# Window attention: the projection as five split float32r products instead of two float32 ones

## The reference, cut to what matters

```python
h = _layernorm(xw, ln1_g, ln1_b)                  # xw: (windows, 64, 192)
qkv = (h @ qkv_w).reshape(-1, N, 3, nh, hd)
q, k, v = (qkv[:, :, 0], qkv[:, :, 1], qkv[:, :, 2])
attn = jax.nn.softmax(jnp.einsum('bnhd,bmhd->bhnm', q, k) * scale, axis=-1)
o = jnp.einsum('bhnm,bmhd->bnhd', attn, v).reshape(-1, N, C)
a = o @ proj_w + proj_b + xw                      # the projection
```

## Time and profile before

| | us |
|---|---|
| median of three runs | 3452.77 (3448.55 to 3457.2) |
| the profiled execution | 3452.14 |
| its span, first to last instruction | 3450.4 |
| mean granted TensorE clock | 0.982 |
| PE busy over the span | 3299.2 (96%) |
| PEld | 3199.6 (93%) |
| DVE | 2625.2 (76%) |
| ACT | 2016.5 (58%) |
| POOL | 1149.2 (33%) |

### The profile page before, as it was taken

The page is one execution under the profiler, slowest core; times in us unless marked ns, Lnnn a source line. Parts: engine busy times, 40 slices in busy tenths (PEclk is TensorE's granted clock), DMA queues, the critical chain, the costliest instruction groups (busy, mean ns, idle before and its releaser), DMA issues. The chain is left out here.

```text
span 3450.4 us, 86941 instructions
## 1 busy us (share of the span) xinstructions
PE 3299.2 (96%) x31288; PEld 3199.6 (93%) x31288; DVE 2625.2 (76%) x6465; ACT 2016.5 (58%) x5410; POOL 1149.2 (33%) x2151
## 2 busy tenths in 40 slices
PE   7999999999799999999978869999999899999999
PEld 6999998899799999999978869989999899989999
DVE  6777777777467676767679989979999788875554
ACT  5777777777344444444436656668999655532222
POOL 4333333333244444444323300014444356630000
PEclk9999999999899999999989989999999999999999
DMA  2677888711012111212178866645555788877775
GB/s 67 183 237 237 259 283 271 254 56 46 22 50 55 48 53 48 56 44 56 48 201 258 265 186 186 199 130 161 169 166 165 211 235 234 236 223 231 226 223 175
DMA packets 473215, 556.40 MB, mean 161 GB/s; under 512 B 78805, under 2 KB 332122, under 8 KB 472794
## 3 DMA queue, kind: packets, MB, share of 16 engines
q1 hardware_dynamic: 447450, 531.57, 51.7%
q10 hardware_dynamic: 25344, 19.27, 1.7%
HBM read 405.31 MB, written 258.67 MB: 192 GB/s over the span
## 5 line engine op out<-in xcount | busy, mean ns | idle before, releaser
L1468 PE MATMUL PS<-dw_grid,dw_mats 128*128 128x196 f32 (+1 forms) x3840 | 627.3, 327 | 34.2 <-DVE dw_mats L1400 34.2
L1468 PEld LDWEIGHTS PS<-dw_grid,dw_mats 128*128 128x128 f32 x3840 | 626.5, 192 | 34.6 <-issue 34.6
L1283 PE MATMUL PS<-mlp_w,mlp_hid 128*128 128x192 f32 x2352 | 414.4, 326 | 0.5 <-ACT mlp_hid L820 0.5
L1396 DVE COPY dw_grid<-X 32x392 f32<-32x392 f32 (+1 forms) x480 | 290.0, 604 | 163.8 <-PE PS L1468 149.6
L1283 PEld LDWEIGHTS PS<-mlp_w,mlp_hid 128*128 128x128 f32 x2352 | 378.6, 190 | 0.8 <-ACT mlp_hid L820 0.8
L1823 PE MATMUL PS<-grn_gain,down_hi 128*128 128x384 f32 x1176 | 353.2, 362 | 10.3 <-POOL X_low L1776 10.3
L820 ACT ACTIVATE mlp_hid<-PS,mlp_b 128x256 f32<-128x256 f32 x588 | 247.5, 472 | 112.1 <-PE PS L811 112.1
L546 ACT ACTIVATE att_vbd<-PS,att_rs 64x96 f32<-64x96 f32 x784 | 264.7, 338 | 12.7 <-DVE att_rows L476 5.4
L1776 POOL TENSOR_TENSOR X_low<-X,down_hi 128x128 fp32r<-128x128 f32 x196 | 208.9, 1066 | 152.5 <-ACT down_hi L1786 152.5
L1134 POOL COPY X<-mlp_x 128x192 f32<-128x192 f32 x196 | 114.7, 585 | 432.5 <-DVE mlp_x L1210 432.0
L1435 ACT ACTIVATE dw_res<-PS,dw_brow 128x196 f32<-128x196 f32 x192 | 81.8, 426 | 298.2 <-PE PS L1468 298.2
(11 more groups left out here) (254 smaller groups left out, 9805.2 us busy)
## 6 DMA issues: line engine op xcount, KB each, us to landing
scratch_hid<-hid_hid SPq DMA_DIRECT2D x196, 320.0 KB, 3.4
down_hid<-scratch_hid SPq DMA_DIRECT2D x196, 320.0 KB, 3.6
scratch_wide<-scratch_taps SPq DMA_DIRECT2D x64, 960.0 KB, 6.1
dw_raw<-scratch_wide SPq DMA_DIRECT2D x96, 640.0 KB, 4.3
scratch_wide<-scratch_taps SPq DMA_DIRECT2D x64, 768.0 KB, 5.5
dw_raw<-scratch_wide SPq DMA_DIRECT2D x96, 512.0 KB, 3.6
scratch_u<-mlp_u SPq DMA_DIRECT2D x56, 378.0 KB, 3.0
att_x<-in_x SPq DMA_DIRECT2D x196, 96.0 KB, 2.3
```

The costliest lines, as they stand in the source:

```text
L1283: last = nc.tensor.matmul(psD[i], hid[:, p.buf(2), m, i * 128:(i + 1) * 128], w2[:, m, :], start=(m == 0), stop=(m == MC - 1))
L1396: last = nc.vector.tensor_copy(dst, src)
L1468: last = nc.tensor.matmul(dst[:, :, ys, :], m, src, start=(i == 0), stop=(i == len(steps) - 1))
```

## The change

The projection is computed from rounded parts. `oh` is `ot` rounded to float32r, `ol` is the rest, and the weights are split in the same way (`wpa` for channels 0 to 127, `wpb` for the other 64). Channels 128 to 191 stand twice in the transposed tile, in partitions 0 to 63 and again in 64 to 127: GpSimd copies these 64 columns of `o` beside themselves (`twice`) so that one product with `wpb` gives high x high and high x low at once. The fifth product has the low part of these channels in partitions 0 to 63, and two rows of ones (64 and 96) against two rows of `wpr`, the bias and its rest. The rounding and splitting is GpSimd's (`halves`). `ot`, `oh` and `ol` have one buffer each, and `xt` has two instead of three. GpSimd now works in every step. The weights' split is made by VectorE in a new function `projection()` at the end of its step 4, and not before the loop. The raw weights and bias are loaded with five DMAs instead of two.

```diff
-    XR, TR = 12, 3
+    XR, TR = 12, 2
...
-    o = s.sb("o", [128, 2, C])
-    ot = s.sb("ot", [128, 2, KC, 128])
+    o = s.sb("o", [128, 2, 256])
+    ot = s.sb("ot", [128, 256])
+    oh = s.sb("oh", [128, 256], F32R)
+    ol = s.sb("ol", [128, 256], F32R)
...
-            sp.dma_start(wp[0:CH, :, :], a["L0_conv_proj_w"].rearrange("(k p) n -> p k n", k=KC)).then_inc(wloaded, 16)
-            sp.dma_start(pbrow[96:97, :], a["L0_conv_proj_b"].partition_broadcast(1)).then_inc(wloaded, 16)
+            for at_, rows_, k in ((slice(0, 128), slice(0, 128), 0), (slice(0, 64), slice(128, C), 1), (slice(64, 128), slice(128, C), 1)):
+                sp.dma_start(wp[at_, k, :], a["L0_conv_proj_w"][rows_, :]).then_inc(wloaded, 16)
+            for r in (64, 96):
+                sp.dma_start(pbrow[r:r + 1, :], a["L0_conv_proj_b"].partition_broadcast(1)).then_inc(wloaded, 16)
...
+            def halves(b):
+                pool.wait_ge(q["ot_ready"], b.n + 1)
+                if b.reached(1):
+                    pool.wait_ge(q["proj"], b.n)
+                else:
+                    pool.wait_ge(q["ones"], 2)
+                nc.gpsimd.tensor_copy(oh[:, :], ot[:, :]).then_inc(q["o_high"], 1)
+                pool.wait_ge(q["o_high"], b.n + 1)
+                nc.gpsimd.tensor_tensor(ol[:, 0:128], ot[:, 0:128], as_f32(oh[:, 0:128]), ALU.subtract).then_inc(q["o_low"], 1)
+                pool.wait_ge(q["o_low"], b.n + 1)
+                nc.gpsimd.tensor_tensor(ol[0:64, 128:256], ot[0:64, 128:256], as_f32(oh[0:64, 128:256]), ALU.subtract).then_inc(q["o_split"], 1)
+                pool.wait_ge(q["o_split"], b.n + 1)
+
+            def twice(b):
+                pool.wait_ge(q["o_ready"], b.n + 1)
+                nc.gpsimd.tensor_copy(o[:, b.buf(2), C:256], o[:, b.buf(2), 128:C]).then_inc(q["o_twice"], 1)
...
+            def body(t):
+                b = t.back(AHEAD + 4)
+                if b.inside(NB):
+                    halves(b)
+                b = t.back(AHEAD + 3)
+                if b.inside(NB):
+                    twice(b)
+                if t.inside(NB) and t.j % 2 == 0:
+                    columns(t.pair())
+                if t.inside(NB) and t.j % 2 == 1:
+                    spread(t)
+            unrolled(NB, LAG, body)
...
-                dve.wait_ge(q["pbias"], 1)
-                nc.vector.tensor_tensor(wp[96:97, 0, :], psPB, pbrow[96:97, :], ALU.add).then_inc(q["weights"], 1)
-                dve.wait_ge(q["weights"], 1)
                 dve.wait_ge(q["split"], 2)
+
+            def projection():
+                for i, r in enumerate((64, 96)):
+                    dve.wait_ge(q["pbias"], 1)
+                    nc.vector.tensor_tensor(pbrow[r:r + 1, :], psPB[i], pbrow[r:r + 1, :], ALU.add).then_inc(q["pb"], 1)
+                nc.vector.tensor_copy(wpa[0][:, :], wp[:, 0, :]).then_inc(q["pw"], 1)
...
+                if t.n == 4:
+                    projection()
...
-                    if b.reached(2):
-                        act.wait_ge(q["proj"], b.n - 1)
-                    nc.scalar.activation(ot[0:CH, b.buf(2), :, :], psOT.rearrange("p (k n) -> p k n", k=KC), ACT.Identity).then_inc(q["ot_ready"], 1)
+                    if b.reached(1):
+                        act.wait_ge(q["o_split"], b.n)
+                    nc.scalar.activation(ot[:, :], psOT, ACT.Identity).then_inc(q["ot_ready"], 1)
...
-                    pe.wait_ge(q["o_ready"], b.n + 1)
+                    pe.wait_ge(q["o_twice"], b.n + 1)
...
-                    for k in range(KC):
-                        last = nc.tensor.transpose(psOT[:, k * 128:(k + 1) * 128], o[:, b.buf(2), k * CH:(k + 1) * CH], ident[:, :])
-                    last.then_inc(q["ot"], 1)
+                    nc.tensor.transpose(psOT[:, 0:128], o[:, b.buf(2), 0:128], ident[:, :])
+                    nc.tensor.transpose(psOT[:, 128:256], o[:, b.buf(2), 128:256], ident[:, :]).then_inc(q["ot"], 1)
...
-                    pe.wait_ge(q["ot_ready"], b.n + 1)
+                    pe.wait_ge(q["o_split"], b.n + 1)
...
-                    nc.tensor.matmul(psPJ, ot[0:CH + 1, b.buf(2), 0, :], wp[0:CH + 1, 0, :], start=True, stop=False)
-                    nc.tensor.matmul(psPJ, ot[0:CH, b.buf(2), 1, :], wp[0:CH, 1, :], start=False, stop=True).then_inc(q["proj"], 1)
+                    else:
+                        pe.wait_ge(q["weights"], 5)
+                    terms = ((oh[:, 0:128], wpa[0][:, :]), (oh[:, 0:128], wpa[1][:, :]), (ol[:, 0:128], wpa[0][:, :]), (oh[:, 128:256], wpb[:, :]),
+                             (ol[0:97, 128:256], wpr[0:97, :]))
+                    for j, (h, w) in enumerate(terms):
+                        last = nc.tensor.matmul(psPJ, h, w, start=(j == 0), stop=(j == 4))
+                    last.then_inc(q["proj"], 1)
```

More of the change, by code:

```diff
@@ L296, in attention @@
     wb = s.parts("wb", [128, W])
-    wp = s.sb("wp", [128, KC, C])
+    wpa = s.parts("wpa", [128, C])
+    wpb = s.sb("wpb", [128, C], F32R)
+    wpr = s.sb("wpr", [128, C], F32R)
     gb = s.sb("gb", [128, 2, 2])
     qkbias = s.sb("qkbias", [128, QK])
-    vbias = s.sb("vbias", [CH, KC])
+    vbias = s.sb("vbias", [128, KC])
     ident = s.sb("ident", [128, 128])
@@ L335, in attention @@
     psMean = [PS[:, i, 0:HALF] for i in range(2)]
-    psVB = PS[0:CH, 7, 0:KC]
-    psPB = PS[96:97, 4, 0:C]
+    psVB = PS[:, 7, 0:KC]
+    psPB = [PS[r:r + 1, 4, 0:C] for r in (64, 96)]
     wloaded, ready, loaded, tloaded = s.sem("wloaded"), s.sem("ready"), s.sems("loaded", 4), s.sems("tloaded", TR)
@@ L341, in attention @@
              "stats", "aggr", "var_ok", "rstd", "h_high", "h_low", "h_ready", "half_a", "half_b", "a_kept", "b_kept", "v_ready",
-             "turned", "qk_ready", "scores", "max", "shifted", "probs", "pt", "pt_ready", "pv", "recip", "o_ready", "ot", "ot_ready",
+             "turned", "qk_ready", "scores", "max", "shifted", "probs", "pt", "pt_ready", "pv", "recip", "o_ready", "ot", "ot_ready", "o_high", "o_low", "o_split", "o_twice", "pb", "pb_high", "pw", "ones",
              "proj", "resid")
     q = {x: s.sem(x) for x in names}
-    LOADS = 3 + 6 + 1 + 1
+    LOADS = 3 + 6 + 3 + 2
     READY = 6 + 4 * 2
@@ L394, in _ @@
             pool.wait_ge(ready, 4)
-            nc.gpsimd.memset(ot[96:97, :, 0, :], 1.0).then_inc(ready, 1)
+            nc.gpsimd.memset(zeros, 0.0).then_inc(ready, 1)
             pool.wait_ge(ready, 5)
@@ L401, in _, with columns @@
             pool.wait_ge(ready, 6)
-            def body(t):
-                if t.j % 2 == 0 or not t.inside(NB):
-                    return
-                u = t.pair()
+            def halves(b):
[13 more added lines that the diff above has]
+                nc.gpsimd.tensor_copy(o[:, b.buf(2), C:256], o[:, b.buf(2), 128:C]).then_inc(q["o_twice"], 1)
+            def columns(u):
                 if u.n == 3:
@@ L420, in body, with spread @@
                 pool.wait_ge(q["h_ready"], u.n + 1)
+            def spread(t):
+                u = t.pair()
                 both = slice(t.buf(4) - 1, t.buf(4) + 1)
@@ L564, in _ @@
             pe.wait_ge(q["wide"], 1)
-            for k in range(KC):
-                m = slice(QK + k * CH, QK + k * CH + CH)
-                nc.tensor.matmul(psVB[:, k:k + 1], raw[:, 0, m], gb[:, 1, 0:1], start=True, stop=False)
-                nc.tensor.matmul(psVB[:, k:k + 1], raw[0:64, 1, m], gb[0:64, 1, 1:2], start=False, stop=True)
+            for k, n in ((0, 128), (1, 64)):
+                m = slice(QK + k * 128, QK + k * 128 + n)
+                nc.tensor.matmul(psVB[0:n, k:k + 1], raw[:, 0, m], gb[:, 1, 0:1], start=True, stop=False)
+                nc.tensor.matmul(psVB[0:n, k:k + 1], raw[0:64, 1, m], gb[0:64, 1, 1:2], start=False, stop=True)
             for out, m in ((psA, slice(0, HALF)), (psB[:, 0:QK - HALF], slice(HALF, QK))):
@@ L578, in _ @@
             last.then_inc(q["mean"], 1)
-            pe.wait_ge(q["bias_kept"], 1)
-            for k in range(KC):
-                last = nc.tensor.matmul(psPB, vbias[:, k:k + 1], wp[0:CH, k, :], start=(k == 0), stop=(k == KC - 1))
+            pe.wait_ge(q["bias_kept"], 2)
+            for out in psPB:
+                nc.tensor.matmul(out, vbias[:, 0:1], wp[:, 0, :], start=True, stop=False)
+                last = nc.tensor.matmul(out, vbias[0:64, 1:2], wp[0:64, 1, :], start=False, stop=True)
             last.then_inc(q["pbias"], 1)
             pe.wait_ge(q["centred"], 4)
-            pe.wait_ge(q["weights"], 2)
+            pe.wait_ge(q["weights"], 1)
             pe.wait_ge(q["split"], 2)
```

26 lines of the change are left out of this document (21 added, 5 removed).

## The result

| | before | after |
|---|---|---|
| median, us (6 runs each, one chip) | 3454.29 (3447.49 to 3458.18) | 3471.17 (3465.59 to 3476.54) |
| ratio | | 1.0052, 95% interval 1.0037 to 1.0068 |
| span of the profiled execution | 3450.4 | 3467.9 |

A forecast was written before the change was run, and what follows sets the result against it. The prediction took TensorE to bound attention. From the profiled 3452.1 us it took 22.6 for shorter steps and added 9.8 paid once, giving 3439.3, so a median of 3440, range 3420 to 3455.

The forecast's parts named there:

- the paragraph on SP: SP's DMA queue: `xt` loads issued about 4.7 us later, still over 12 us before use; nothing booked.
- the paragraph on GpSimd: GpSimd in attention: load 3.4 of 4.14 us per block, TensorE's copy 1.3 us to spare; nothing booked.
- The products: TensorE's projection: five float32r products at 0.112 us shorten each step by 0.12 us, 22.6 us over 188 steps.
- Rival A: TensorE's projection: stationary operand loads hide, five products cost 0.09 us each; 3423 us, chance 0.18.
- Rival C: GpSimd bounds every step, its two subtractions slowed by contention to 1.10 us each; 3592 us, chance 0.07.
- What is paid once: Set-up and pipeline filling: 1.1 set-up, 3.0 `projection()`, 4.2 GpSimd insertions, 1.5 clock; 9.8 us in all.
- The set-up: Before the loop: three more DMA issues delay the start, less L455 leaving its end; cost 1.1 us.
- the two insertions on GpSimd: GpSimd's steps 6 and 10: clearing of tables costs about 2.4 us, preparation about 1.8, together 4.2.
- the clock: TensorE's start: three new stalls, each with one chance in three of about 1.7 us at lower clock; 1.5 booked.
- Rival B: Gain spent: products at 0.116 us each, start costs 12 to 15 us through lower clock; 3450 to 3453, chance 0.17.

The follow-up runs named there:

- e2: The changed kernel with each expansion issued right behind the load of `x`, ahead of the `xt` loads: 3444.0 us, ratio 0.9976 to before.
- e16: e4 with the load of a pair's `xt` moved a step later on SP: 3428.1 us, ratio 0.992 to before.
- e17: The changed kernel with only the load of `xt` moved a step later on SP: 3452.43 us, ratio 1.0002 to before.
- e3: The changed kernel with table clearing, table preparation and most of the weights' split moved to earlier places: 3464.92 us, ratio 1.0034 to before.
- e5: The kernel before with both expansions of a pair of steps issued back to back in the odd step: 3467.66 us, ratio 1.0033.
- e15: e12 with the changed kernel's GpSimd work added on a tile of its own, for which nobody waits: 3485.05 us, ratio 1.0086 to before.
- e12: The kernel before with e2's order on SP and two `xt` buffers instead of three: 3446.3 us, ratio 0.9977.
- e7: The changed kernel with all 128 expansions issued after the loop of attention: 3746.57 us, ratio 1.0841 to before; only attention is compared.
- e13: e4 with a sixth product in the projection: 3452.8 us, ratio 0.9997 to before.
- e4: The changed kernel with the edits of e2 and e3 together: 3437.42 us, ratio 0.9954 to before.

## Why the prediction was wrong

**The step that failed** is the paragraph on SP, "Nothing is booked". It looked at what the delayed load of `xt` and the loads of `x` are needed for, and both were in time indeed. It did not list the expansions among what is queued behind the new wait, nor ask what their bunching would disturb. Nor did the paragraph on GpSimd follow its new place of the rounding, 6.5 us after the step's start, into SP's wait. What the runs showed in its place: the excess rose from 11.7 to 40.8, 29 us of a miss of 31; the start has 1.0 more (below), and the steps 0.8. Changes to SP's order and waits show the cause: e2, e16 and e17 on the changed kernel (-27, and -43 with e3's edit, and -19), e5 and e15 on the kernel before (+14, and +39 over e12, of which 6 are a stop at 128 us), and e7, in which the changed kernel does not stop from 135 us on until its expansions start, at 827. That a late piece of the program is the link between the two is read from the DMA records beside each stop; no run changed it by itself.

**The products** came out as forecast: 0.116 us a step against 0.12, with 0.11 a product. The parts of the sum were less exact than the sum: the group starts 0.13 us behind the first transpose (0.22 was booked), its first distance is 0.17 and not 0.11, and from the last product to L695 pass 0.21 (0.18). TensorE: Matmul & The Clock Gate, a page of the Trainium skill, gives about P/1.2 ns for a load of P columns (section LDWEIGHTS), an estimate of 107 ns here; by that the loads set the pace, and the 108 to 113 ns agree, while the 82.5 ns, which the page gives for a product alone (section Back-to-back issue gap), do not appear. Rival A is out.

**GpSimd** was right in its sizes, 0.455 and 0.449 against 0.46, and in that TensorE never waits for it in a full step. Rival C is out. Its busy time in the 200 us is 137.3; 140 was forecast.

**What is paid once** was forecast at 9.8. TensorE's step 14 starts at 68.79 us before and at 81.66 after; with the six short steps until then the changed kernel has paid 13.6. But the kernel before pays in its steps 14 to 16 for VectorE's tables and for the low clock of the earlier trace rows. By step 17 (86.82 and 96.56), nine short steps included, 10.8 are left, 1.0 over the forecast, and e3, which starts step 17 at 85.99, takes 10.6 of them back. The set-up cost 0.9 (1.1). Behind `projection()` TensorE waited 3.66 (3.0), and behind the two insertions on GpSimd 2.17 and 1.54, together 3.7 (4.2):

```profile
39.55 1.12 PE L719 MATMUL PS<-att_ident,att_rows 128*128 128x128 f32 x4 [3.66 <-DVE att_rows L531]
```

```profile
53.32 0.33 PE L671 MATMUL PS<-att_ident,att_o 128*128 128x128 f32 x1 [2.17 <-POOL att_o L426]
...
73.14 0.33 PE L671 MATMUL PS<-att_ident,att_o 128*128 128x128 f32 x1 [1.54 <-POOL att_o L426]
```

The rest is 5.3 us at step 14 and 2.5 at step 17, against 1.5 booked for the clock; no run separates what the clock has in it. Each of the three stalls came with a stretch at the lower level, where one chance in three had been booked (windows as in the earlier trace rows; before, only the third place had one):

```profile
38.00:42.00 4.00, 2.45 (x11) 2.45 (x12) 3.15 (x9) 2.39 (x6) 0.94 (x2) 0.50 0.14 42
42.00:46.00 4.00, 4.00 (x66) 3.60 (x64) 2.39 (x7) 2.33 (x7) 0.44 (x4) 0.70 0.09 24
54.00:57.00 3.00, 3.00 (x58) 2.69 (x58) 2.19 (x6) 1.66 (x6) 2.41 (x7) 0.61 0.30 80
...
75.00:78.00 3.00, 3.00 (x33) 2.93 (x15) 2.65 (x7) 1.78 (x4) 2.70 (x7) 0.52 0.15 38
```

**Rival B** (the gain is spent) came nearest, but stopped 18 us short of the result and had the start as its reason and not SP. A slower kernel had 0.10 of the chances, for other reasons. With both mended, e16 against e12, two buffers of `xt` and no gap under 3.2 us in both, the change is worth 18 of the 22 us that the products were to bring: step 195 starts at 833.79 against 852.79.

**Open** is why the same number of close pairs costs more in one kernel than in another: 63 cost before 27 us, 41 cost after 41, 48 cost e15 36. In the latter two an `xt` load and an `x` load leave in the same burst. Nor do the records show what delays a piece of code, only that it comes late. That the short step or denser code (D) counts as well where the expansions are crowded is suggested by e13 and not shown. The four kernels with no gap under 3.2 us have 4.5 to 5.5 us, whatever their code, step or buffers, which leaves D little room where SP is even.

## What to carry to other kernels

When a change delays an engine, follow every semaphore of that engine into the DMA queue, and list all that is queued behind the wait, above all large background transfers that nobody seems to wait for. Put a load that waits for late work behind the transfers that need no wait, and a step later, so that the queue is paced by one wait a step; either alone left 17 to 19 us of excess here (e2, e4, e17), both together 5.5 (e16). Where TensorE stops at "issue" in a run of products without semaphores, look for its cause among the DMAs: here it was the program itself arriving late.

## What was not expected of the hardware

This long unrolled program is fetched while it runs, TensorE's in 257 pieces of 16 KB before and 259 after, and large data transfers issued close together hold it up. The average DMA share told nothing: from 400 to 600 us e16 moves more than after, 294 GB/s against 269 (0.90 against 0.81), and does not stall. Trainium Architecture — The Big Picture, a page of the Trainium skill (section The software stack), tells of instruction streams brought to the engines at load; here they come during the run, one piece per 7.2 us.

Three of the stops after, which end at 242, 524 and 651 us, were followed by a stretch at the lower clock (granted 0.53 from 243 to 246 us, 0.50 in the 3 us below, 0.60 from 653 to 656), so these stops of 2.2 to 2.8 us cost more than themselves. Stops as long, at 366, 445 and 571 us, were not. Before, there was no such stretch between 100 and 889 us.

```profile
526.00:529.00 3.00, 3.00 (x15) 2.98 (x14) 1.22 (x4) 1.55 (x4) 0.00 (x0) 0.50 1.02 343
```
